# A four-layer graph network on one core: layer 4's maps from three f16 and float32r products in place of fp32's

## The reference, cut to what matters

```
def _sage_conv(x, src, dst, Wl, Wr, b):
    agg = segment_sum(x[src], dst);  deg = segment_sum(1, dst)
    mean = agg / maximum(deg, 1.0)[:, None]
    return mean @ Wl + x @ Wr + b

h = maximum(_layernorm(x), 0)                      # 3125 x 256
h = relu(_sage_conv(h, Wl1, Wr1, b1))              # 256 -> 256
h = relu(_sage_conv(h, Wl2, Wr2, b2))              # 256 -> 128
h = relu(_sage_conv(h, Wl3, Wr3, b3))              # 128 -> 256
return x + _sage_conv(h, Wl4, Wr4, b4)             # 256 -> 256
```

## Time and profile before

| | us |
|---|---|
| median of 3 runs | 666.85 |
| lowest, highest | 663.74, 667.23 |
| span of the profiled execution, first to last instruction | 659.6 |
| median less that span | 7.25 |

### The profile page before, as it was taken

The page is one execution under the profiler, slowest core; times in us unless marked ns, Lnnn a source line. Parts: engine busy times, 40 slices in busy tenths (PEclk is TensorE's granted clock), DMA queues, the critical chain, the costliest instruction groups (busy, mean ns, idle before and its releaser), DMA issues.

```text
span 659.6 us, 10093 instructions
## 1 busy us (share of the span) xinstructions
PE 622.7 (94%) x4071; PEld 345.0 (52%) x4072; DVE 276.2 (42%) x526; ACT 179.1 (27%) x381; POOL 42.8 (6%) x91
## 2 busy tenths in 40 slices
PE   5679998899999899998999999899999999999998
PEld 4436555555554455553444444444445555646686
DVE  6978877678788779711212121111120100101011
ACT  3886854265643623210111011121110000000000
POOL 8002300000000000000000000000001011010110
PEclk9977999999999999999999999999999999999999
DMA  8301200510231122242534431445430223032030
GB/s 265 95 0 49 79 1 2 183 51 6 69 33 52 34 52 65 50 136 48 160 87 117 122 85 45 101 111 144 120 121 1 54 70 112 0 112 83 30 113 33
DMA packets 63526, 50.98 MB, mean 77 GB/s; under 512 B 35510, under 2 KB 48347, under 8 KB 63480
## 3 DMA queue, kind: packets, MB, share of 16 engines
q1 hardware_dynamic: 63124, 49.74, 26.6%
q0 software_dynamic: 240, 0.37, 0.2%
q10 hardware_dynamic: 116, 0.24, 0.1%
HBM read 28.15 MB, written 16.60 MB: 68 GB/s over the span
## 4 chain that ended last, share of the span: by engine, by line
PE 78%; DMA 7%; DVE 7%; ACT 3%; issue 2%; SPq 1%; POOL 1%; DVEq 0%; ACTq 0%; POOLq 0%
PE agg_ps L2241 27%; PE window_ps L2241 18%; PE lin_ps L2159 6%; PE lin_ps L2176 5%; PE window_ps L2072 4%; PE lin_ps L2135 3%; DMA rdeg_d<-newH 3%; PE lin_ps L2029 2%; PE window_ps L2217 2%; PE agg_ps L2217 2%; DMA rdeg_d<-rdeg 2%; DVE early L1445 1%; PE lin_ps L2263 1%; ACT counts L1794 1%; PE lin_ps L2184 1%
## 5 line engine op out<-in xcount | busy, mean ns | idle before, releaser
L2241 PE MATMUL agg_ps<-counts,H 128*128 128x512 f16 (+3 forms) x1026 | 235.0, 355 | 1.6 <-DVE aggT L1536 1.5
L2241 PEld LDWEIGHTS agg_ps<-counts,H 128*128 128x128 f16 (+1 forms) x1026 | 79.2, 98 | 56.6 <-issue 10.8
L1794 ACT ACTIVATE counts<-window_ps 128x400 f16<-128x400 f32 x150 | 73.6, 507 | 64.5 <-PE window_ps L2072 50.6
L1438 DVE TENSOR_TENSOR counts<-early 128x2048 f16<-128x2048 bf16 x66 | 77.9, 1215 | 6.3 <-PE window_ps L2072 4.8
L2241 PE MATMUL window_ps<-counts,early 128*128 128x512 f16 (+2 forms) x346 | 77.6, 379 | 0.0
L2241 PEld LDWEIGHTS window_ps<-counts,early 128*128 128x128 f16 (+1 forms) x346 | 33.7, 98 | 41.5 <-issue 3.4
L2241 PE MATMUL window_ps<-counts,H 128*128 128x512 f16 (+2 forms) x291 | 55.3, 346 | 0.0
L1536 DVE SCALAR_TENSOR_TENSOR aggT<-agg_ps,columns,rdeg 128x512 f32<-128x512 f32 (+1 forms) x27 | 16.9, 659 | 81.2 <-PE agg_ps L2241 62.6
L2072 PEld LDWEIGHTS window_ps<-counts 128*128 128x128 f16 x412 | 30.8, 99 | 34.3 <-issue 4.6
L1438 DVE TENSOR_TENSOR early<-early 128x1024 f16<-128x1024 bf16 (+1 forms) x69 | 43.8, 684 | 7.4 <-PE window_ps L2072 5.9
L2241 PE MATMUL agg_ps<-counts,early 128*128 (+4 forms) x297 | 46.5, 314 | 0.0
(11 more groups left out here) (241 smaller groups left out, 631.9 us busy)
## 6 DMA issues: line engine op xcount, KB each, us to landing
selfT<-hT_d SPq DMA_DIRECT2D x18, 512.0 KB, 4.2
hT_d<-newT SPq DMA_DIRECT2D x12, 512.0 KB, 4.5
rdeg<-rdeg_d SPq DMA_DIRECT2D x22, 256.0 KB, 4.1
counts<-in_x_dram SPq DMA_DIRECT2D x6, 512.0 KB, 7.9
hT_d<-counts SPq DMA_DIRECT2D x6, 512.0 KB, 3.4
newH<-in_x_dram SPq DMA_DIRECT2D x6, 512.0 KB
out_dram<-newT SPq DMA_DIRECT2D x5, 512.0 KB
hT_d<-newT SPq DMA_DIRECT2D x6, 256.0 KB, 3.9
```

The source lines that it names most:

```text
L1438: v.tensor_tensor(hots_of(group).rearrange("p r a (n d) -> p r a n d", d=2), pairs.unsqueeze(1).unsqueeze(1).broadcast_to([P, n, 2, P // 2 ...
L1794: a.activation(counts[:, :, 2 * w * WIN:2 * (w + 1) * WIN].rearrange("p t (a w) -> p a t w", a=2), window_bank(FILL_AT[w])[:, 0:2 * KEYS]. ...
L2241: last = m((agg_ps, window_ps)[bank][:, h, 0:n], tile[:, part, h * P:(h + 1) * P], counts[0:rows_, k, chunk_cols(c, n)], start=first and p ...
```

## The change

In layer 4, for all places but the last, an operand h is split as high and low f16 parts and the weights likewise, and the product is put together from three: high by high, low by low (both f16, accumulated in one PSUM region `[:, 0:D]`), and the sum of the parts by the sum of the parts (float32r, in `[:, D:2D]` of the same bank). Per tile of 128 nodes this is 8 f16 products and 4 float32r products of 256 columns in place of 4 float32 ones.

```diff
-                for g, (at, k) in enumerate(((0, 2), (2, 2)) if n == CH else ((0, 1),)):
-                    dve.wait_ge(lin_done[4], both(q, 2, 1) + g + 1)
-                    v.tensor_tensor(... two tiles of lin_ps + x4 ...).then_inc(out_made, 1)
+                for i in range(t):
+                    dve.wait_ge(lin_done[4], both(q, TPC, 1) + i + 1)
+                    ins = v.scalar_tensor_tensor(out=o[0:rows_, i, :], in0=last_ps(i)[0:rows_, 0:D],
+                                                 scalar=unscale_high[0:rows_, :], in1=x4[0:rows_, i, :], ...)
+                order.after(ins)
+                for i in range(t):
+                    v.scalar_tensor_tensor(out=o[0:rows_, i, :], in0=last_ps(i)[0:rows_, D:2 * D],
+                                           scalar=unscale_sum[0:rows_, :], in1=o[0:rows_, i, :], ...
+                                           ).then_inc(out_made, 1)
+            def split_weights():                                              # DVE, once
+                dve.wait_ge(W4_parts, 2)
+                dve.wait_ge(agg_done[3], NCH)
+                for of in range(2): ... W4_rest = W14 * 32 - W4_high          # 128x512
+                dve.wait_ge(lin_done[3], 2 * NCH)
+                dve.wait_ge(turn_copied[3], turned_before(3, NCH))
+                for of in range(2): ... W4_sums = W4_rest * 2048 + W4_high    # float32r
+                for of in range(2): ... W4_rest = W4_sums - W4_high ... .then_inc(W4_rests, 1)
+            def split_operand(of, q):                                         # DVE
+                for k in range(2):
+                    dve.wait_ge(operand_high, 4 * q + 2 * (1 - of) + k + 1)
+                    ins = v.scalar_tensor_tensor(out=last_sums[:, of, k, 0:n], in0=last_high[:, of, k, 0:n],
+                                                 scalar=1 - SPLIT, in1=whole[:, k, 0:n], ...)
+                order.after(ins)
+                for k in range(2):
+                    v.tensor_tensor(last_low[of][:, k, 0:n], last_sums[...], last_high[...], ALU.subtract
+                                    ).then_inc(operand_low, 1)
             def place(q, bank):                                               # DVE
+                    if l == 4: split_operand(1, q)
                     scale_agg(l, q, bank)
+                    if l == 4: split_operand(0, q)
-                    place(0, FIRST_BANK[l]); over_places(dve, place, ...); place(NCH - 2, ...)
+                for q in range(NCH if l < 4 else NCH - 1): place(q, ...)      # written out, no loop
+            def operand_parts(of, q):                                         # ACT
+                for k in range(2):
+                    (waits self_loaded[4] for of = 1, agg_scaled[4] of half k for of = 0)
+                    a.activation(last_high[:, of, k, 0:n], last_from[of][:, k, 0:n], ACT.Copy, scale=1 / SPLIT
+                                 ).then_inc(operand_high, 1)
+            act.wait_ge(late_loaded, LATE); act.wait_ge(lin_done[2], NCH)
+            (ACT: W4_high x2 of 128x512; after W4_rests, W4_low x4 of 128x256)
+            for q in range(NCH - 1):
+                operand_parts(1, q)
+                operand_parts(0, q)
+            def last_maps(q):                                                 # PE, in place of lin(4, q)
+                if isinstance(q, int) and q == 0:
+                    pe.wait_ge(W4_parts, 6)
+                pe.wait_ge(operand_low, 4 * (q + 1))
+                if not isinstance(q, int) or q > 0:
+                    pe.wait_ge(out_made, both(q, TPC, 1))
+                for i in range(t):
+                    node, wide = slice(i * P, i * P + rows_), slice(i * P, (i + 1) * P)
+                    products = [(part[:, node], w) for of in (1, 0) for k in range(2)
+                                for part, w in ((last_high[:, of, k, :], W4_high[of][:, k, :]),
+                                                (last_low[of][:, k, :], W4_low[of][k]))]
+                    for j, (h, w) in enumerate(products):
+                        m(last_ps(i)[0:rows_, 0:D], h, w, start=(j == 0), stop=(j == len(products) - 1))
+                    for j, (of, k) in enumerate(((1, 0), (1, 1), (0, 0), (0, 1))):
+                        last = m(last_ps(i)[:, D:2 * D], last_sums[:, of, k, wide], W4_sums[of][:, k, :], ...)
+                    last.then_inc(lin_done[4], 1)
-                        4: {4: [lambda: lin(4, q)]}}[l]
+                        4: {8: [lambda: lin(4, q)]}}[l]
-                        4: {2: [lambda: lin(4, 0)], 10: [lambda: lin(4, 1)]}}[l]
+                        4: {2: [lambda: lin(4, 0)], 12: [lambda: lin(4, 1)]}}[l]
```

More of the change, by code:

```diff
@@ L278, in sage_stack_kernel @@
         counts = sb("counts", [P, NT, NPAD], f16)
+        with nc.sbuf_tensor("last_sums", [P, 2, 2, CH], f32r) as last_sums:
+            pass
         H = sb("H", [P, NT, 2, D], f16)
@@ L324, in sage_stack_kernel @@
         minus_one = sb("minus_one", [P, 2], f16)
+        with nc.sbuf_tensor("W4_sums_own", [P, 2, D], f32r) as W4_sums_own:
+            pass
         plan_all = sb("plan", [P, 2 * NWIN], i32)
@@ L334, in sage_stack_kernel @@
         newT = sb("newT", [P, 2, CH], f32)
+        with nc.sbuf_tensor("W4_sums_agg", [P, 2, D], f32r) as W4_sums_agg:
+            pass
         partsT = sb("partsT", [P, 2, CH], f16)
@@ L338, in sage_stack_kernel @@
         ident16 = sb("ident16", [P, P], f16)
[L339 removed]
+        columns = sb("columns", [P, 18], f32)
         bT = columns[:, 0:5]
@@ L342, in sage_stack_kernel @@
         unscale = columns[:, 8:12]
+        scale_up, bias3_up = columns[:, 12:13], columns[:, 13:15]
+        unscale_high, unscale_sum, unscale_up = (columns[:, i:i + 1] for i in (15, 16, 17))
         upper = newH[:, TPC // 2:TPC, :, :].rearrange("p t h f -> p (t h f)")
@@ L591, in sage_stack_kernel @@
         x4_biased = sem("x4_biased")
-        last_products = [sem(f"last_products_{i}") for i in range(TPC)]
+        last_products = sem("last_products")
+        LAST_PRODUCTS = (6, 8, 15, 16)
+        W4_parts = sem("W4_parts")
+        W4_rests = sem("W4_rests")
+        operand_high = sem("operand_high")
+        operand_low = sem("operand_low")
         out_made = sem("out_made")
-        rows_made = [sem(f"rows_made_{i}") for i in range(TPC)]
+        rows_made = sem("rows_made")
         out_stored = sem("out_stored")
@@ L642, in sage_stack_kernel @@
         second_parts = raw[:, HALF:HALF + 2 * CH].rearrange("p (a b) -> p a b", a=2)
+        SPLIT = 2.0 ** 11
+        W4_UP = 32.0
+        SUMS_END = 2 * 2 * CH * 2
+        last_high = raw[:, SUMS_END:SUMS_END + 4 * CH].rearrange("p (o k n) -> p o k n", o=2, k=2)
+        BEHIND = WR2 + (NT - IN_EARLY) * 2 * D
+        assert WR2 == 2 * D and SUMS_END + 4 * CH + D <= HALF and BEHIND + 3 * D <= early.shape[-1]
+        last_low = [tile[:, :, :].rearrange("p a b -> p (a b)").bitcast(f16)[:, 0:2 * CH].rearrange(
+            "p (k n) -> p k n", k=2) for tile in (aggT, selfT)]
+        last_from = [aggT, selfT]
+        W4_sums = [W4_sums_agg, W4_sums_own]
+        W4_high = [early[:, at:at + 2 * D].rearrange("p (k n) -> p k n", k=2) for at in (0, BEHIND)]
+        spare_low = Wl2_sb[:, :, :].rearrange("p k n -> p (k n)").bitcast(f16)
+        W4_low = [[spare_low[:, 0:D], spare_low[:, D:2 * D]],
+                  [raw[:, SUMS_END + 4 * CH:SUMS_END + 4 * CH + D], early[:, BEHIND + 2 * D:BEHIND + 3 * D]]]
+        W4_rest = raw[:, 0:2 * 4 * D].bitcast(f32).rearrange("p (o k n) -> p o k n", o=2, k=2)
         def in_second(l, q, h):
@@ new lines, in split_weights @@
+            def split_weights():
+                dve.wait_ge(W4_parts, 2)
+                dve.wait_ge(agg_done[3], NCH)
+                for of in range(2):
+                    ins = v.scalar_tensor_tensor(out=W4_rest[:, of, :, :], in0=W14[:, of, :, :], scalar=W4_UP,
+                                                 in1=W4_high[of], op0=ALU.mult, op1=ALU.subtract)
+                order.after(ins)
+                dve.wait_ge(lin_done[3], 2 * NCH)
+                dve.wait_ge(turn_copied[3], turned_before(3, NCH))
+                for of in range(2):
+                    ins = v.scalar_tensor_tensor(out=W4_sums[of][:, :, :], in0=W4_rest[:, of, :, :], scalar=SPLIT,
+                                                 in1=W4_high[of], op0=ALU.mult, op1=ALU.add)
+                order.after(ins)
+                for of in range(2):
+                    v.tensor_tensor(W4_rest[:, of, :, :], W4_sums[of][:, :, :].bitcast(f32), W4_high[of], ALU.subtract
+                                    ).then_inc(W4_rests, 1)
@@ new lines, in split_operand @@
+            def split_operand(of, q):
+                n, t = size_of(chunk_at(q))
+                whole = last_from[of]
+                for k in range(2):
+                    dve.wait_ge(operand_high, 4 * q + 2 * (1 - of) + k + 1)
```

(12 more changed lines are left out.)

72 lines of the change are left out of this document (55 added, 17 removed).

## The result

| | kernel before | changed kernel |
|---|---|---|
| median, us (5 runs each) | 663.74 | 652.57 |
| lowest, highest | 659.12, 667.23 | 651.41, 657.7 |
| span of the profiled execution | 659.6 | 655.9 |
| time of the profiled execution | (not listed) | 657.7 |

Three executions of the kernel before in the later timings (669.82, 671.32 and 3350.48 us) count as slow and enter no ratio.

What follows compares the result with a forecast made beforehand. Layer 4 was taken as a queue of TensorE (PE) products, PE busy 94%. Terms: -8.2 - 0.5 + 0.7 + 0.1 = -7.9 us, from the median 666.85 to 658.9 us; range 656 to 667.7, the forecast's own 656.5 to 661.5 at 70%.

Steps and rivals of the forecast that it cites:

- the level it was put on: Last step of the sum: 7.9 us taken from the earlier median 666.85, not from the profiled span 659.6, giving 658.9.
- Full tiles: Layer 4 maps, places 0, 2, 3, 4 and 5: 20 tiles of 1.318 us for 1.728, 8.2 us saved.
- The tail: Place 1's tile of 53 nodes: the same 12 products, 1.32 us for 1.86, 0.5 us saved.
- The stall at place 5: PE waits for the low parts before place 5's maps: 0.7 us lost, bounds 0.3 and 1.5.
- The end: Behind the last product, `add_last` becomes a scalar_tensor_tensor, 478 ns for 424, two in a row: 0.1 us lost.
- No waits at places 0 to 4, the outputs and weights hidden: Operand splits ready before PE at places 0 to 4, longer output adds and weight splitting covered: nothing lost.
- The rival with the load standing out (201 ns): Float32r weight load not hidden: tile 1.677 us, 666.5 us in all; 11% together with the double-pass case.
- that with two cycles a column (216): Float32r takes a double pass: tile 1.737 us, 667.7 us in all; 11% together with the unhidden-load case.
- The slower rival: Layer 4's 84 float32r products run at float32's rate, 432 ns each: 19.0 us slower, 685.9 us; 9%.
- The late chain: Split operands reach PE late at places 0, 1 and 5, stalls 1, 1 and 2 us: 662.2 us; 10%.

Runs made afterwards that it cites:

- the second timing: Changed kernel, no edit, timed again in alternation with the kernel before: 658.45 against 666.64 us, ratio 0.9872.
- the third: Changed kernel timed a third time, no edit, against the kernel before: 656.66 against 663.24 us, ratio 0.9892.
- the later position: Changed kernel with place 5's maps after step 13 of the last place's first half, not step 8: 658.87 against 667.66 us, ratio 0.9884.
- the float32 experiment: Changed kernel with the products of the sums of parts read as float32, same bytes: 684.83 us in one execution, stretch 186.05 us.
- the all-f16 kernel: Changed kernel with float32r products replaced by f16 high-by-low and low-by-high, low by low left out: 653.71 against 666.64 us, ratio 0.9837; again 654.91 against 663.24, 0.9872.
- 84 more: Changed kernel with each tile's four float32r products issued twice: 665.15 us in one execution, stretch 169.84 us.

## Why the prediction was right in its mechanism and wrong in its number

**The step that failed is the last one of the sum, the level it was put on**: "Taken from the median: 666.85 - 7.9 = 658.9 us". The median of three runs was taken as the level on which the next timing would stand, 7.25 us above the profiled span. Every later run shows a time of 1.75 to 1.94 us above its own span (657.7 and 655.9; 662.05 and 660.3). The profiled execution of before was thus one of about 661.4 us, an estimate from these pairs, and against it, as the working began, the sum gives 653.5, 0.9 from the median of the first timing. That it comes so near is in part luck, as the gain was 0.6 smaller and the set's mix of runs could have been another.

Of the 6.4 us between 658.95 and 652.57, 3.1 are the fall of the kernel before's own median, from 666.85 in three runs to 663.74 in five, and 3.3 are a timed difference of 11.2 for 7.9. Neither lies in the maps. The spread of before, 3.5 us over three runs, had been seen, but it went into the range as noise of one sign or the other on 658.9, not as runs of different clock, mostly 5 to 6 us apart: the range had no room for a set of five with four at the upper clock. In the second timing, where the kernel before stood at 666.64, the changed one's median was 658.45, almost the 658.9 forecast; in the third it was 656.66.

**The gain.** Forecast 7.9, in the stretch 7.30. By its terms:
- *Full tiles, 8.2 forecast, 7.35 measured.* Here the term was mis-sized: a tile is 1.36 us, not 1.318. A float32r product costs 116 to 119 ns, not 111; of the two rows that I had, 111 and 116, I took the lower. And f16 products behind float32r ones cost 111 for 109.
- *The tail, 0.5 forecast, 0.2 to 0.3 measured* (1.65 for 1.86, and the pieces around it). The float32r products load 128 columns for 53 nodes, and the change of shape shows below.
- *The stall at place 5, 0.7 forecast, 0.23 measured* (the later position). Place and releaser were right (a DVE low part); the chain took 4.06 us where I had 4.5, as two DVE steps take 1.30 us, not 1.41 to 1.5, and ACT's first 0.64.
- *The end, 0.1 forecast, 0.01 measured*: `add_last` is longer by 0.08, and the scaling before it shorter by 0.06.
- *No waits at places 0 to 4, the outputs and weights hidden*: right. The chain names PE alone there.

8.7 - 0.8 - 0.3 - 0.2 = 7.4, with 7.30 measured.

**The rivals.** The rival with the load standing out (201 ns) and that with two cycles a column (216) are excluded by 116; whether the 7 ns over f16 are the longer load's, no run tells. By the rule of the Trainium skill ("TensorE: Matmul & The Clock Gate", "What overlaps and what doesn't") that a weight load overlaps running products only where the row group differs, the 188 ns load would have stood out; the trace disagrees, for float32r as for float32. The slower rival's price is right (26 us), and it doesn't hold. The late chain did not come; its mechanism shows at place 0, where it was covered: DVE's split ran beside GpSimd's bias. DVE, then POOL, of the changed kernel in order of time; the last line is the same four POOL instructions in the float32 experiment, which has no split:

```profile
499.94 1.83 DVE L1733 SCALAR_TENSOR_TENSOR last_sums<-H,selfT 128x512 fp32r<-128x512 f16 x2 [1.32 <-ACT H L2038]
501.80 2.23 DVE L1737 TENSOR_TENSOR selfT<-last_sums,H 128x512 f16<-128x512 f32 x2
508.91 1.29 DVE L1733 SCALAR_TENSOR_TENSOR last_sums<-H,aggT 128x512 fp32r<-128x512 f16 x2
```

```profile
499.29 4.19 POOL L1134 TENSOR_TENSOR newH<-newH,plan 128x256 f32<-128x256 f32 x4 [214.35 <-DMA newH<-in_x_dram]
...
537.18 2.78 POOL L1134 TENSOR_TENSOR newH<-newH,plan 128x256 f32<-128x256 f32 x4 [9.23 <-DMA newH<-in_x_dram]
```

```profile
499.43 2.77 POOL L1134 TENSOR_TENSOR newH<-newH,plan 128x256 f32<-128x256 f32 x4 [215.35 <-DMA newH<-in_x_dram]
```

Beside each other the two DVE pairs took 1.83 and 2.23 us for 1.29 alone, and the four POOL instructions 4.19 for 2.77 or 2.78. In the second profile of the changed kernel POOL was done at 504.48, and the second DVE pair, from 505.67, took 1.29. The Trainium skill ("Advanced Engine Details and Errata", "GPSIMD Details") says that GpSimd shares a read and a write interface with DVE and conflicts with DVE instructions of two SBUF inputs; the trace agrees.

**What stays open.** Why TensorE's clock falls after the wait at 105 us in one execution and not in the next, with the same wait, no run tells. And the first timing's interval ends at 0.9882, just under the 0.989 that 7.3 us are; the later ones (0.9872, 0.9892) hold it. I put the rest down to the mix of runs, as the table of clocks suggests, but no timing repeats that mix, and the clocks of the kernel before's first five runs aren't on record: for the 3.9 us this is argued, not shown.

## What to carry to other kernels

Put the sum on the profiled execution's own time, and before that look how far the runs of the kernel lie apart and whether their clocks differ: here the mean granted clock of a run sorts them, by 3 to 6 us, which is most of what the change is worth. A stretch of the trace that is bound by one engine repeats to 0.01 us, where medians of five to eleven runs moved by 4 to 6; such a stretch tells variants apart that no timing can. When a float32 product is to be made of parts, high by low and low by high in f16 was cheaper than sums in float32r: as many products, 109 ns for 116, and a shorter chain to make the operands.

## What the runs showed of the hardware that was not expected

- A float32r product of 256 columns with a fresh 128-column load costs 116 to 119 ns (84 more cost 9.78 us), f16 109, float32 432 (1.73 us for four).
- A scale given as a constant is quicker than one from a column: two `scale_agg` of 512 columns 1.41 us with the column, 1.29 with the constant; ACT's high part 0.71 us and 0.62. Layer 3's Relu with a scale column added went from 0.69 to 0.78.
- A change of the stationary operand's width costs TensorE 0.1 to 0.2 us. After the tail's 53-column loads, in the second profile of the changed kernel, TensorE's weight loads in order of time:

```profile
531.30 0.30 PEld L2267 LDWEIGHTS lin_ps<-W_sums_own,last_sums 128*128 128x128 f32 x2 [0.20 <-issue]
```

  In the chain the tail's 4 float32r products, behind the narrow loads, take 0.66 us, a full tile's 0.48; its 8 f16 products, behind the sums' wide ones, 0.99 for 0.87 to 0.89. The change of type isn't needed for it: in the all-f16 kernel the tail's first four products take 0.55 us for 0.44, and the 46 sums behind the tail 10.04 for the 9.95 that they take in the changed kernel behind wide loads.
